# Attention with transposed scores: keys on partitions, sums of exponentials by matmul, row maxima from an extra pass of scores

## The reference

```python
t = tokens * rsqrt(mean(tokens * tokens, -1) + eps) * rms_w
gates = sigmoid(t @ w_gates)                  # one number per token and head
q = einsum('bnd,hde->bhne', t, wq); k = ...wk; v = ...wv
score = einsum('bhie,bhje->bhij', q, k) * scale
score = where(causal_mask, -max_float, score)
attn = softmax(score, axis=-1)
out = einsum('bhij,bhje->bhie', attn, v) * gates
pred_values = einsum('bhne,hed->bnd', out, wo)
x = layernorm(tokens + pred_values)           # what follows reads x
```

## Time and profile before

| | us |
|---|---|
| median of 3 runs | 725.47 (723.32 to 726.62) |
| the profiled execution's own time (its span) | 723.0 |
| PE busy | 627.0 |
| PE weight loads busy | 511.7 |
| DVE busy | 485.0 |
| ACT busy | 417.0 |
| POOL busy | 116.4 |

### The profile page before, as it was taken

How to read it: one execution, slowest core, us unless ns; L and a number is a source line. 1 busy time by engine, 2 the same in 40 slices (tenths; PEclk the granted TensorE clock), 3 DMA queues, 4 the chain that set the end, 5 groups by cost and what they waited for, 6 DMA issues and landing times.

```text
span 723.0 us, 14787 instructions
## 1 busy us (share of the span) xinstructions
PE 627.0 (87%) x5300; PEld 511.7 (71%) x5300; DVE 485.0 (67%) x1556; ACT 417.0 (58%) x909; POOL 116.4 (16%) x229
## 2 busy tenths in 40 slices
PE   4899999999999999999999999998766079999930
PEld 2688888778888868888886888887623047888830
DVE  4788776698776778876768887767771033665636
ACT  4876566786655687665668766565330012655636
POOL 2000000000000000000000000000327600677630
PEclk9999999999999999999999999999599579999975
DMA  6600000130000040000007920003821100222233
GB/s 152 140 2 1 2 1 3 44 75 1 3 1 1 2 105 14 1 2 2 1 2 166 127 2 2 1 2 124 227 16 52 51 23 11 74 79 78 64 98 105
DMA packets 56393, 33.57 MB, mean 46 GB/s; under 512 B 23809, under 2 KB 49665, under 8 KB 56321
## 3 DMA queue, kind: packets, MB, share of 16 engines
q1 hardware_dynamic: 53760, 27.37, 18.8%
q0 software_dynamic: 2560, 5.26, 2.2%
HBM read 14.75 MB, written 9.48 MB: 34 GB/s over the span
## 4 chain that ended last, share of the span: by engine, by line
PE 74%; DVE 12%; another core or an unknown queue 5%; ACT 3%; issue 2%; DMA 2%; SPq 1%; POOL 0%; DVEq 0%; ACTq 0%; POOLq 0%
PE ps_t L966 18%; PE ps_o L1079 18%; PE ps_s L1048 11%; PE ps_s L1050 9%; PE ps_s L1198 5%; PE ps_o L1089 4%; PE ps_o L1186 3%; DVE k_l L671 3%; DVE q_hl L671 2%; PE ps_s L1122 2%; PE ps_t L1133 1%; PE ps_s L974 1%; ACT k_h L500 1%; DMA act_s<-y_rows 1%
## 5 line engine op out<-in xcount | busy, mean ns | idle before, releaser
L966 PE MATMUL ps_t<-ident,probs 128*128 128x128 f32 x1104 | 173.4, 275 | 11.6 <-ACT probs L512 11.5
L966 PEld LDWEIGHTS ps_t<-ident,probs 128*128 128x128 f32 x1104 | 134.9, 141 | 48.5 <-issue 11.4
L543 ACT ACTIVATE probs<-probs,nmax 128x128 f32<-128x128 f32 (+15 forms) x128 | 153.6, 1200 | 21.1 <-DVE nmax L766 12.4
L775 DVE COPY probsT<-ps_t 128x512 f32<-128x512 f32 (+3 forms) x160 | 91.3, 570 | 101.4 <-PE ps_t L966 100.4
L554 ACT ACTIVATE probsT<-ps_t 128x512 f32<-128x512 f32 (+3 forms) x160 | 89.7, 561 | 98.5 <-PE ps_t L966 97.1
L1048 PE MATMUL ps_s<-k_h,q_hl 128*128 128x512 f32 (+3 forms) x320 | 142.3, 448 | 0.4 <-DMA k_l<-k_l 0.4
L1079 PE MATMUL ps_o<-probsT,v_sb 128*64 128x128 f32 x2176 | 140.0, 277 | 1.3 <-DVE x_acc L790 1.2
L1079 PEld LDWEIGHTS ps_o<-probsT,v_sb 128*64 128x64 f32 x2176 | 116.8, 137 | 19.6 <-issue 14.6
L761 DVE TENSOR_SCALAR_CACHE_REDUCE probs<-ps_s 128x512 f32<-128x512 f32 x192 | 128.4, 686 | 0.7
L1050 PE MATMUL ps_s<-k_l,q_hl 128*128 128x512 f32 (+3 forms) x320 | 117.0, 366 | 0.0
L429 POOL TENSOR_TENSOR rden<-rsum,gate 128x2 f32<-128x2 f32 x64 | 12.6, 197 | 403.9 <-ACT probs L543 392.6
(11 more groups left out here) (144 smaller groups left out, 738.8 us busy)
## 6 DMA issues: line engine op xcount, KB each, us to landing
k_h<-k_h SPq DMA_DIRECT2D x32, 128.0 KB, 2.4
k_l<-k_l SPq DMA_DIRECT2D x32, 128.0 KB, 2.3
w_all<-in_L_ffn_W SPq DMA_DIRECT2D x2, 2048.0 KB, 12.6
xg<-x_sorted SPq DMA_DIRECT2D x48, 64.5 KB
x_sorted<-zeros SPq DMA_DIRECT2D x12, 256.0 KB, 9.5
act_s<-y_rows SPq DMA_DIRECT2D x8, 256.0 KB, 5.4
x_acc<-in_L_attn_tokens SPq DMA_DIRECT2D x4, 256.0 KB, 3.8
out<-x_acc SPq DMA_DIRECT2D x4, 256.0 KB, 2.3
```

The costliest lines, as they stand in the source:

```text
L543: nc.scalar.activation(probs[s % 2][h][:, 0:w], probs[s % 2][h][:, 0:w], ACT.Exp, bias=nmax[:, row], scale=-1.0, accum_out=rsum[:, row]).t ...
L775: nc.vector.tensor_copy(probsT[s % 2][h][:, c * BT:c * BT + w // P, :].rearrange("p n i -> p (n i)"), ps_t[1][:, 0:w]).then_inc(moved1, 1)
L966: return nc.tensor.transpose(dst, src, ident[:, :])
```

## The change

The attention is written anew in terms of **items** and **steps**. An item is a pair of heads and a group of 512 queries (16 items, of 4, 8, 12 and 16 steps in each pair). A step is one tile of 128 keys against the 512 queries, both heads: 160 steps. In the last four steps of an item only 512, 384, 256 and 128 columns are left below the diagonal. Two steps make a burst, and there are 80 bursts.

- `scores`: PE computes k times q with **keys on partitions**, plain float32 (two records), head 0 on rows 0 to 63 of the array and head 1 on rows 64 to 127, each head into its own bank. Two more matmuls of rounded operands (L1120) subtract the query's maximum.
- `exps`: ACT takes the exponential of 128x1024 numbers out of PSUM into a ring of four tiles. The tiles are what the matmul with v reads (L1137), with 512 columns: no transposes, no copies of turned blocks.
- On diagonal tiles POOL zeroes what is masked (`cut`). The sums over keys are kept by DVE (even steps) and POOL (odd steps), joined by DVE (`combine`), and summed over partitions by 8 matmuls with a column of ones (`sums`, L1090).
- `look`: the maxima come from an extra pass of scores, queries on partitions, one matmul of rounded operands for each head and chunk; DVE reduces each look (L711, L715, L721). There are 160 looks, all into the one tile `ps_two` of two banks, which `times_out` also uses. They run up to `AHEAD` = 20 looks ahead. PE turns the maxima into rows (`turn_m`).
- `unload`, `times_out`, `add_out`: ACT copies 128x512, PE multiplies with wo into `ps_two`, ACT copies 128x1024 to `o_sb`, DVE adds.
- No high and low parts and no DMA copies of k. ACT writes k and q twice (rounded and whole). 41 projections stand in the loop, seven before it (`START`).
- The norms of the first three groups of tokens stand in the last bursts. `w_all` is loaded when the last maxima have been turned.

```diff
-    PLACE = {"scores": -0.15, "turn": 1.0, "times_v": 0.77, "times_wo": 0.6, "project": 0.0}
+    ITEMS = [(p, g) for p in range(PAIRS) for g in range(NC)]
+    LEN = [BT * (g + 1) for _, g in ITEMS]
+    STEPS = [(i, j) for i in range(len(ITEMS)) for j in range(LEN[i])]
+    BURSTS = len(STEPS) // 2
+    RING = 4
+    AHEAD = 20
...
+    for b in range(BURSTS):
+        upto = min(len(LOOKS), max(done, min(done + 4, 2 * b + 2 + AHEAD)))
+        units = list(range(done, upto))
+        looks_at.append((units[:len(units) // 2], units[len(units) // 2:]))
...
+            for b in range(BURSTS + 1):
+                for s in (2 * b - 2, 2 * b - 1):
+                    if s in pool_add_of:
+                        add(s)
+                for s in (2 * b, 2 * b + 1):
+                    if s in diagonals:
+                        cut(s)
...
+            def exps(s):
+                act.wait_ge(step_done, s + 1)
+                if s in ring_of:
+                    if ring_of[s] >= RING:
+                        was = ring_steps[ring_of[s] - RING]
+                        act.wait_ge(pv_done, was + 1)
...
+                nc.scalar.activation(probabilities(s)[:, :, cols], ps_step[s % 2][:, :, cols], ACT.Exp,
+                                     scale=SCALE).then_inc(exp_done, 1)
...
+            for b in range(BURSTS):
+                exps(2 * b)
+                exps(2 * b + 1)
+                for i in range(len(ITEMS)):
+                    if LAST_B[i] + 2 == b:
+                        times_out(i)
+                    if LAST_B[i] + 1 == b:
+                        unload(i)
...
+                if c < g:
+                    nc.vector.tensor_reduce(c_max[:, tile % 4, :, c], ps_two[:, :, :], X, ALU.max).then_inc(look_done, 1)
+                    return
...
+            def free_double(x):
+                if double_of[x]:
+                    was, k = DOUBLE[double_of[x] - 1]
+                    pe.wait_ge(look_done if was == "look" else o_ready, k + 1)
...
+                for h in range(2):
+                    nc.tensor.matmul(ps_step[s % 2][:, h, cols], k_t[p % 2][head_rows(h), j * P:(j + 1) * P],
+                                     q_t[head_rows(h), at:(g + 1) * BANK], start=True, stop=False)
+                for h in range(2):
+                    mm = nc.tensor.matmul(ps_step[s % 2][:, h, cols], minus[head_rows(h), :], m_row[head_rows(h), g, cols],
+                                          start=False, stop=True)
...
+            for b in range(BURSTS):
+                for n in looks_at[b][0]:
+                    look(n)
+                scores(2 * b)
+                scores(2 * b + 1)
+                for i in range(len(ITEMS)):
+                    if LAST_B[i] + 2 == b:
+                        times_out(i)
+                for n in looks_at[b][1]:
+                    look(n)
+                if b:
+                    times_v(2 * b - 2)
+                    times_v(2 * b - 1)
+                for x in single_at[b]:
+                    single(x)
```

More of the change, by code:

```diff
@@ L45, in attention_moe_layer @@
     MASKED = -1e30
[L49 to L56, removed]
+    ITEMS = [(p, g) for p in range(PAIRS) for g in range(NC)]
+    LEN = [BT * (g + 1) for _, g in ITEMS]
+    FIRST = [sum(LEN[:i]) for i in range(len(ITEMS))]
@@ new lines, in attention_moe_layer @@
+    NORM_B = LAST_B[-2] + 4
+    NORMED = NC - 1
+    for c in range(NORMED):
+        if NORM_B + 3 + c < BURSTS:
+            single_at[NORM_B + 3 + c].append(("turn_x", c))
+    SINGLE_TAIL = [("turn_x", NORMED - 1), ("sums", len(ITEMS) - 1), ("logits", 0), ("turn_x", NORMED), ("logits", NORMED)]
+    SINGLE = [("turn_m", 0)] + [x for units in single_at for x in units] + SINGLE_TAIL
+    assert len(set(SINGLE)) == len(SINGLE)
+    on_vector = ("sums", "logits")
+    act_of = {x: n for n, x in enumerate(x for x in SINGLE if x[0] not in on_vector)}
@@ L486, in _, with keep @@
         def _(act):
[L487 to L490 removed]
+            def keep(w, p, c, bank):
+                cols = slice(c * BANK, (c + 1) * BANK)
                 if w == V:
[L492 to L502 removed]
@@ L820, in _ @@
+            combine(len(ITEMS) - 1)
+            for c in range(NORMED):
+                if NORM_B + 2 + c >= BURSTS:
+                    norm(c)
+            factors(len(ITEMS) - 1)
+            add_out(len(ITEMS) - 1)
+            spread((NORMED,))
+            inverse((NORMED,), 2)
+            norm(NORMED)
+            largest_logits(range(NORMED), ("logits", 0))
+            largest_logits((NORMED,), ("logits", NORMED))
             for k in range(TOPK):
@@ new lines, in look @@
+            def look(n):
+                i, t, c = LOOKS[n]
+                p, g = ITEMS[i]
+                w = BANK if c < g else (t + 1) * P
+                if t == 0:
+                    if c == 0:
+                        wait_projected(pe, Q, p, g)
+                    wait_projected(pe, K, p, c)
+                free_double(("look", n))
+                for h in range(2):
+                    at = (g * BT + t) * P
+                    mm = nc.tensor.matmul(ps_two[:, h, 0:w], q_r[head_rows(h), at:at + P],
+                                          k_r[p % 2][head_rows(h), c * BANK:c * BANK + w], start=True, stop=True)
+                mm.then_inc(double_fill, 1)
@@ new lines, in times_out @@
+            def times_out(i):
+                p, g = ITEMS[i]
+                pe.wait_ge(outT_ready, i + 1)
+                if i == 0:
+                    pe.wait_ge(wo_in, 16)
+                free_double(("out", i))
+                for t in range(BT):
+                    for h in range(2):
+                        mm = nc.tensor.matmul(ps_two[:, h, t * D:(t + 1) * D], outT[head_rows(h), i % 2, t * P:(t + 1) * P],
+                                              wo_sb[head_rows(h), p, :], start=True, stop=True)
+                mm.then_inc(double_fill, 1)
```

985 lines of the change are left out of this document (495 added, 490 removed).

## The result

The changed kernel takes **773.29 us** (771.93 to 774.17, four runs), the kernel before 725.25 beside it: ratio 1.0658, 95% interval 1.0633 to 1.0683. It is 6.6% slower. The forecast was slower by 2.4% (743), with a range of 700 to 785. The direction was right and the time is inside the range, but of 48 us the forecast had 18. Where the other 30 come from is the subject of what follows.

The account below looks back on a forecast made before the run. The prediction took PE to bound the attention loop. Start 35, loop 494 (418 of PE work, 76 of waits), end 24 and rest 187 gave 740, and 743 us as a median 2.5 above the profiled execution; range 700 to 785.

Parts of the forecast that it names:

- Start: Before the loop: first scores at 35 us, bounds 31 to 39, against 32.5 in the kernel before.
- Scores at 1.09 a step: In the loop: both heads' score matmuls run fully at once on two halves of the rows, 148 us in all.
- one after the other: Rival on the loop's scores: the two halves of the rows don't run at once; 880 us, chance 0.13.
- half at once: Rival on the loop's scores: a step costs 1.29 us instead of 1.09, 27 us more; 770 us, chance 0.09.
- PE's own work at full clock: In the loop: PE's work without waits sums to 418 us, 55 less than the loop had before.
- The waits: In the loop: PE waits 76 us for round trips through `ps_two`, 26 of them in bursts 0 to 7.
- half as long: Rival on the loop's waits: 38 us instead of 76; 705 us, chance 0.26; below 58 us of waits, faster than before.
- PE's share of each part lies on the path: In the loop: PE is the bound, so its time for each part counts in full; 418 us together.
- busy time over 450: Sign in the loop: the forecast is wrong if PE's busy time there exceeds 450 us.
- POOL 2.3 us by twice 1174 ns: In the loop: POOL's addition of 1024 numbers every second step takes 2.3 us and hides behind PE if bursts last 5.
- the end: From the last v product to the first scatter: 24 us, bounds 20 and 31, against 30.9 before.
- statistics 1.5, root and inverse 0.8: In the last norm behind the loop: these two pieces take 1.5 and 0.8 us of the 24.

Follow-up runs that it names:

- e13: Changed kernel plus three unread 512-column matmuls between the two looks of each back-to-back pair in bursts 0 to 7; ratio 1.0554 to the kernel before.
- e8: Changed kernel with POOL's four additions for `shared` all waiting for the last normed group; ratio 1.0674 to the kernel before.
- e1: Changed kernel with POOL's 60 additions to the partial sums cut from up to 1024 numbers per partition to 2; ratio 1.0535 to the kernel before.
- e9: Changed kernel with DVE's addition of the gated output to `x_acc` moved behind the second look of its burst; 789.7 and 794.3 us beside 725.8.
- e6: Changed kernel with the product with wo moved behind the second look of its burst; ratio 1.0759 to the kernel before.

## Why the prediction was right or wrong

The sum was 740 us of span; 770.7 were measured, a slowdown of 6.6% where 2.4% was forecast. The excess by stretches: start -0.8, loop +26.6, end +5.9, rest -1.0.

- **Start**: forecast 35, measured 34.2. Right.
- **Scores at 1.09 a step, the halves of the rows at once**: right, to the hundredth. The rivals "one after the other" (880) and "half at once" (770) fall, though the measured time is near the latter: the agreement is chance.
- **PE's own work at full clock**: right within some us. A burst without looks takes 4.25 us (burst 75), which is 2 x 1.09 + 2 x 0.86 + 0.36 = 4.26. For bursts 8 to 79 the forecast had 422 with the waits, measured 426.0, of which some 1.6 are the clock in burst 61 (10.48 us at 0.84; in e13 8.86 at 1.00).
- **The waits**: forecast 76 us in the loop. PE's idle time is 520.6 - 458.7 = 62, and there are 52 waits ahead of a look of over 0.3 us, each with a tail of PE in front of it that counts as busy (0.2 us as an estimate, from a look's 0.50 us of record against 0.34 from its start to the next unit's): 72. In the first eight bursts 25.2 us idle against 26. Ahead of L1053, DVE's reads ended 35 us of idle in the loop where the prediction looked for 45, and `o_sb` 16 in 14 places where it looked for 20. The mechanism holds, and the size is somewhat under the forecast; "half as long" is refuted, if narrowly, as the idle time is above its 58.
- **The step that failed first**: "PE's share of each part lies on the path", priced by rows that were all taken at a clock of 1.00. The prediction put 26 us of waits into the first eight bursts and left PE's 46 us beside them unchanged. The waits lowered the clock to 0.75, and PE's busy time there was 69.4. e13 shows 9 to 13 us of this (against e8 and against the changed kernel); the rest of the 22.6 stays open. The prediction's own sign of being wrong, busy time over 450, was the one that came (458.7).
- **The second**: "POOL 2.3 us by twice 1174 ns, if that is not slowed by DVE". The prediction asked whether DVE slows POOL, not the other way round. The one slowed is DVE: the addition priced at 1.2 takes 2.08, and that is 8.5 us in bursts 8 to 79 (e1). Without it they would stand at 417.5, under the forecast's 422: that the forecast for them is off by 4.0 only is in part luck, as the waits came out shorter and the additions longer.
- **The third**: the end, 24 against 29.9. The term "statistics 1.5, root and inverse 0.8" was mis-sized by the 3.6 us for which POOL's additions hold DVE (e8). Another 1.0 is the sum over partitions, which the list of the end left out: `o_sb` is there at 557.8, the factor only at 558.8. Some 1.3 stay open.
- **Rest**: 186.0 against 187.

In short, 743 + 22.6 (of which 9 to 13 shown to be the clock) + 4.0 + 5.9 - 1.8 = 773.7.

## What to carry to other kernels

A wait of PE can cost twice: its length, and what the clock takes from PE's work around it (in e9, 2.2 us and 1.6 more); so price PE's work in a stretch with dense waits at a lower clock, and don't take its rows from a stretch without waits. Additions on GpSimd are not free help for VectorE when both read SBUF: the instruction beside them took 2.08 us instead of 1.23 on average or, where it was small, the whole length of the others (3.81 instead of 0.17). Where one tile and one in-order reader close a loop with PE, moving units about in the reader's queue moves the wait, while shortening the read (here 1.22 to 0.18 us) removes it.

## What the runs showed of the hardware that was not expected

- The clock fell with quite short waits. In the first eight bursts of the changed kernel PE was busy 73% of the time and its longest wait was 1.8 us, yet the mean granted clock was 0.75. The same loop with the same idle time had 0.82 in e8. In e6 one burst ran at 0.58, with PE busy 89% of it.
- A DVE instruction on 4 numbers a partition took 3.81 us beside three POOL additions of 1.16 us each, and 0.17 without them: here DVE got no turn between POOL instructions that follow each other directly.
- During the 32 scatters ACT stands still for about 34 us in both kernels (35.7 us before, 33.6 after), and DVE for 34.0 and 30.6, on the chips where the kernel before takes 726 us. Where it takes 684, the same scatters, 0.97 us each, run beside both engines: the way from the first scatter to the experts is 45 us instead of 74, and the experts take 100 instead of 112. (In e9, on a chip of the first kind, ACT stood still for 17.1 us only, and the way was 64.) The cause stays open. The wait in the changed kernel:

```profile
ACT sil_s L621 <- remote: 33.6, 1, 33.6
```
